# Dense experts of a two-layer decoder on one core: every product taken from coarse and fine parts, down products run beside up products

## What is computed

```python
x_attn = _layernorm(x_flat, ln_g, ln_b) @ attn_w + attn_b + x_flat
g = x_attn.reshape(2, 8, 128, 256)                      # 16 tiles of 128 tokens, 2 per expert
h = gelu(einsum('metd,edf->metf', g, w1) + b1)          # up, width 1024
y = einsum('metf,efd->metd', h, w2) + b2                # down, width 256
out = gelu(y @ next_w + next_b)                         # added to x and normalized after it
```

## Time and profile before

| | us |
|---|---|
| median of 3 runs | 2444.74 |
| lowest and highest of them | 2443.32, 2446.77 |
| profiled execution: span, its own time as far as the profile has it | 2451.3 |
| PE busy in the span | 2287.7 (93%) |
| POOL busy in the span | 1062.9 (43%) |
| stage_f in the profiled execution, first to last work | 1569.3 to 1741.2 |
| of it the opening | 1569.3 to 1596.4 |
| of it experts and tail | 1596.4 to 1741.2 |

### The profile page before, as it was taken

The page is one execution under the profiler, slowest core; times in us unless marked ns, Lnnn a source line. Parts: engine busy times, 40 slices in busy tenths (PEclk is TensorE's granted clock), DMA queues, the critical chain, the costliest instruction groups (busy, mean ns, idle before and its releaser), DMA issues.

```text
span 2451.3 us, 34108 instructions
## 1 busy us (share of the span) xinstructions
PE 2287.7 (93%) x12918; PEld 1434.3 (59%) x12918; DVE 1509.6 (62%) x2293; ACT 1106.9 (45%) x2365; POOL 1062.9 (43%) x780
## 2 busy tenths in 40 slices
PE   6999999989988999999999999999899789979998
PEld 3333343367754555554655555787666657768887
DVE  6778678457744666665666676722344566565556
ACT  1567657733322444443344444332321467643323
POOL 2446546624443788884578786333301122100000
PEclk8899999999999999999999999999899899989999
DMA  6454333232110011112010111254300601020001
GB/s 127 120 98 87 73 68 74 64 90 48 1 18 1 11 15 15 15 28 44 1 15 11 15 15 20 78 159 103 86 2 25 154 24 45 1 65 14 1 1 35
DMA packets 137613, 114.21 MB, mean 47 GB/s; under 512 B 74501, under 2 KB 114931, under 8 KB 137065
## 3 DMA queue, kind: packets, MB, share of 16 engines
q1 hardware_dynamic: 100297, 111.08, 16.7%
q0 software_dynamic: 36864, 0.15, 4.3%
q10 hardware_dynamic: 288, 0.79, 0.2%
HBM read 85.99 MB, written 13.39 MB: 41 GB/s over the span
## 4 chain that ended last, share of the span: by engine, by line
PE 73%; DMA 11%; DVE 8%; ACT 4%; issue 2%; SPq 2%; POOL 0%; ACTq 0%; DVEq 0%; POOLq 0%
PE PS L128 70%; DMA adj<-e_EE,e_IX 8%; SPq L154 2%; PE PS L1248 1%; DVE a_MX L741 1%; DVE c_MX L1896 1%; ACT a_P L847 1%; DVE g_SS L132 1%; DMA a_KS<-a_KL 1%; DMA a_r<-a_RQ 1%; PE PS L360 1%; DVE c_AC L132 1%; DVE g_st L1339 0%; ACT g_SS L1433 0%; PE PS L361 0%
## 5 line engine op out<-in xcount | busy, mean ns | idle before, releaser
L353 POOL DMA_INDIRECT adj<-e_EE,e_IX x256 | 416.9, 1629 | 400.8 <-DMA adj<-e_EE,e_IX 345.9
L1896 DVE TENSOR_REDUCE c_MX<-PS 128x2 f32<-128x1024 f32 x256 | 313.0, 1222 | 176.2 <-PE PS L128 176.2
L132 POOL TENSOR_TENSOR c_AC<-c_AC,c_P 128x1024 f32<-128x1024 f32 x145 | 364.3, 2513 | 77.6 <-DVE c_AC L132 70.5
L1993 ACT ACTIVATE c_P<-PS 128x1024 f32<-128x1024 f32 x256 | 252.0, 1026 | 214.8 <-PE PS L128 214.8
L741 DVE TENSOR_REDUCE a_MX<-PS 128x2 f32<-128x1024 f32 x256 | 303.2, 1219 | 55.3 <-PE PS L128 54.2
L847 ACT ACTIVATE a_P<-PS 128x512 f32<-128x512 f32 x512 | 270.6, 601 | 87.2 <-PE PS L128 86.4
L128 PE MATMUL PS<-c_P,c_VV 128*64 128x512 f32 x1024 | 247.7, 605 | 0.0
L137 POOL TENSOR_SCALAR e_EQ<-e_KR,e_KC 128x128 bf16<-128x128 f32 x256 | 162.8, 636 | 159.4 <-DMA e_KR<-adj_key 121.5
L128 PE MATMUL PS<-a_QS,a_KS 64*128 64x512 f32 x512 | 194.3, 461 | 20.9 <-ACT a_P L847 8.8
L128 PEld LDWEIGHTS PS<-a_QS,a_KS 64*128 64x128 f32 x512 | 84.1, 189 | 172.2 <-ACT a_P L847 96.8
L128 PE MATMUL PS<-a_KS,a_QS 48*128 48x512 f32 x512 | 171.3, 477 | 10.0 <-DMA a_QS<-a_QH 4.8
(11 more groups left out here) (496 smaller groups left out, 4589.7 us busy)
## 6 DMA issues: line engine op xcount, KB each, us to landing
e_KR<-adj_key SPq DMA_DIRECT2D x64, 256.0 KB, 3.9
f_W<-in_L_ffn_w SPq DMA_DIRECT2D x16, 1024.0 KB, 7.5
c_RB<-c_r SPq DMA_DIRECT2D x58, 128.0 KB, 2.8
g_FB<-in_fside_1x16xSxS SPq DMA_DIRECT2D x8, 616.0 KB, 8.6
a_QS<-a_QH SPq DMA_DIRECT2D x32, 128.0 KB, 3.9
adj<-e_zt SPq DMA_DIRECT2D x16, 256.0 KB, 4.2
adj<-e_EE,e_IX POOLq DMA_INDIRECT x256, 3.2
d_AJ<-adj SPq DMA_DIRECT2D x8, 512.0 KB, 9.0
```

Source lines behind the costliest of these rows:

```text
L132: return v.e.tensor_tensor(o, a, b, op)
L353: g.e.indirect_dma_start(self.adj, bass.IndirectOffsetOnAxis(ap=self.IXE[:, k:k + 1], axis=0), self.EE[:, k:k + 1], None, compute_op=ALU.a ...
L1896: v.e.reduce_max(MX[:, w % 2, :, qt, kh], bank(0, 2).rearrange("p (h n) -> p h n", h=2), AX, negate=True).then_inc(*smax_dve.up())
L1993: s.e.activation(PB[t % NP][:, :, :].rearrange("p h n -> p (h n)"), bank(2 + 2 * (t % 2), 2), ACT.Exp, scale=0.125).then_inc(*st_act.up())
```

## The change

Each fp32 product of the experts becomes three products of fp32r operands: coarse x coarse, fine x coarse, coarse x fine. Coarse is the operand cast to fp32r, fine is what is left. The coarse parts are made by casts on ACT; the fine parts by subtractions, on DVE for the activations, `W1` and `NW`, on POOL for `W2` (job `split2`). Two `h` blocks of 128 features form one job now (P = 0 to 31, four per expert), and a down job `y` P - 2 follows up job `h` P, so that down products accumulate over four jobs while up products go on. The two `o` jobs of an expert become one.

In the opening the bias add moves from DVE to POOL (`at_pool` in place of `at_dve`). The 44 `send` calls of POOL are spread over its list: one behind each of the 16 bias adds, one at each of the first 28 `y` jobs. The load of `W1` now waits for up products (`h_pe`), that of `W2` for down products (`y_pe`). The `xt` transposes of the last expert, their banks and the `landmarks` sums (job `marks`) find new places.

```diff
 (schedule)
+            if i in (8, 12):
+                yield "split1", 0, i // 4 - 2
+            if i == 16:
+                yield "split_n",
+        for P in range(34):
+            e, p = divmod(P, 4)
+            if P < 32:
+                yield "h", P
+                if p < 2:
+                    yield "split2", e, p
+                elif e < 7:
+                    yield "split1", e + 1, p - 2
+            if P == 32:
+                yield "marks", 0
+            if P >= 2:
+                yield "y", P - 2
+            if P == 33:
+                yield "marks", 1
+            if p == 2 and e:
+                yield "o", e - 1
+            if P == 26:
                 yield "root", 0
+            if 29 <= P < 33:
+                for n in range(3):
+                    yield "xt", 3 * (P - 29) + n
+        yield "o", 7
 (tensor)
             elif kind == "turn_g":
-                pe.wait_ge(at_dve, t + 1)
+                pe.wait_ge(at_pool, t + 1)
...
             elif kind == "h":
+                pe.wait_ge(w1l_dve, 2 * e + p // 2 + 1)
+                pe.wait_ge(gl_dve, 16)
+                for f in (2 * p, 2 * p + 1):
+                    parts = [(W, G, k) for k in range(2) for W, G in ((W1H, 0), (W1L, 0), (W1H, 1))]
...
             elif kind == "y":
+                pe.wait_ge(w2l_pool, 2 * e + p // 2 + 1)
+                pe.wait_ge(hl_dve, P + 1)
+                for d in range(2):
+                    parts = [(W, h, j) for j in range(2) for W, h in ((W2H, HTH), (W2L, HTH), (W2H, HTL))]
...
 (vector)
-                v.wait_ge(a_dve, t + 1)
-                v.wait_ge(rows_in, 2)
-                tt(v, TM[:, t % 4, :], TM[:, t % 4, :], AB[:, :], ALU.add).then_inc(*at_dve.up())
...
+            elif kind == "h":
+                v.wait_ge(hh_act, P + 1)
+                tt(v, HTL[P % 4][:, :, :], HT[P % 4][:, :, :], HTH[P % 4][:, :, :].bitcast(F32),
+                   ALU.subtract).then_inc(*hl_dve.up())
 (scalar)
+            elif kind == "split2":
+                s.wait_ge(w2_in[e % 2], e // 2 + 1)
+                s.e.copy(W2H[e % 2][:, fs, :], W2[e % 2][:, fs, :]).then_inc(*w2h_act.up())
 (gpsimd)
-        K.edges.send(g, 44)
+        for job in jobs:
+            kind, *a = job
+            if kind == "a":
+                g.wait_ge(rows_in, 2)
+                g.wait_ge(a_dve, t + 1)
+                tt(g, tm, tm, AB[:, :], ALU.add).then_inc(*at_pool.up())
+                K.edges.send(g, 1)
+            elif kind == "split2":
+                g.wait_ge(w2h_act, 2 * e + i + 1)
+                tt(g, W2L[e % 2][:, fs, :], W2[e % 2][:, fs, :], W2H[e % 2][:, fs, :].bitcast(F32),
+                   ALU.subtract).then_inc(*w2l_pool.up())
+            elif kind == "y" and a[0] < 28:
+                K.edges.send(g, 1)
 (sync)
-                sp.wait_ge(y_pe, 2 * (e - 1))
+                sp.wait_ge(h_pe, 8 * (e - 1))
             dma(sp, W1[e % 2][:, :, :], ...)
+            if e > 1:
+                sp.wait_ge(y_pe, 4 * (e - 1))
             dma(sp, W2[e % 2][:, :, :], ...)
```

More of the change, by code:

```diff
@@ L2152, in stage_f @@
     W2 = [sb(c, f"f_W2{i}", [128, 8, 256]) for i in range(2)]
-    HT = [sb(c, f"f_HT{i}", [128, 8, 256]) for i in range(2)]
-    YT = [sb(c, f"f_YT{i}", [128, 2, 256]) for i in range(2)]
+    W1L = [K.over(f"f_W1L{i}", f"f_W1{i}", 0, [128, 2, 1024]) for i in range(2)]
+    W2L = [K.over(f"f_W2L{i}", f"f_W2{i}", 0, [128, 8, 256]) for i in range(2)]
+    W1H = [K.over(f"f_W1H{i}", "a_QH", 8192 * i, [128, 2, 1024]) for i in range(2)]
+    W2H = [K.over(f"f_W2H{i}", "a_QH", 16384 + 8192 * i, [128, 8, 256]) for i in range(2)]
+    NW = sb(c, "f_NW", [128, 2, 256])
+    NWL = K.over("f_NWL", "f_NW", 0, [128, 2, 256])
+    NWH = sb(c, "f_NWH", [128, 2, 256], F32R)
+    HT = [sb(c, f"f_HT{i}", [128, 2, 256]) for i in range(4)]
+    HTL = [K.over(f"f_HTL{i}", f"f_HT{i}", 0, [128, 2, 256]) for i in range(4)]
+    HTH = [sb(c, f"f_HTH{i}", [128, 2, 256], F32R) for i in range(4)]
+    YTH = [sb(c, f"f_YTH{i}", [128, 2, 256], F32R) for i in range(2)]
+    YTL = [sb(c, f"f_YTL{i}", [128, 2, 256], F32R) for i in range(2)]
     TN = sb(c, "f_TN", [128, 4, 256])
@@ L2164, in stage_f @@
     cc_pe, cc_dve, sd_act, n_dve, nt_pe, nt_act = K.signals(6)
-    a_pe, a_dve, at_dve, gt_pe, gt_act = K.signals(5)
-    h_pe, h_act, y_pe, y_dve, o_pe, o_dve, gelu_act, sum_dve = K.signals(8)
+    a_pe, a_dve, at_pool, gt_pe, gt_act, gl_dve = K.signals(6)
+    w1h_act, w1l_dve, w2h_act, w2l_pool, nwh_act, nwl_dve = K.signals(6)
+    h_pe, h_act, hh_act, hl_dve, y_pe, yh_dve, yl_dve, o_pe, o_dve, gelu_act, sum_dve = K.signals(11)
     var_dve, root_act, x_dve, xt_pe, xt_act, xl_dve = K.signals(6)
-    gt_pair = [GT[:, k, :].rearrange("p (m t) -> p m t", m=2) for k in range(2)]
+    gt_pair = [[G[:, k, :].rearrange("p (m t) -> p m t", m=2) for k in range(2)] for G in (GH, GL)]
     SA = K.SA
     by_half = SA[:, :, :].rearrange("p (m e) n -> p m e n", m=2)
+    x_pair = X[:, :, :].rearrange("p (m e) d -> p m e d", m=2)
     tiles = [e + 8 * m for e in range(8) for m in range(2)]
@@ L2205, in xt_bank @@
     def xt_bank(n):
-        return 7 if n < 12 else (7, 0, 1, 2)[n - 12]
+        return (0, 1)[n % 2] if n > 13 else 7 if n < 3 else (3, 4)[n % 2]
     def tensor(_):
@@ L2241, in tensor @@
-                pe.wait_ge(cc_dve, 1)
[L2242 to L2249, removed]
-            elif kind == "y":
[L2251 to L2257, removed]
+                P, = a
@@ L2258, in tensor @@
                 ins.then_inc(*y_pe.up())
             elif kind == "o":
-                e, m = a
-                pe.wait_ge(y_dve, 2 * (e + 1))
-                pe.wait_ge(nw_in, 1)
+                e, = a
+                pe.wait_ge(yl_dve, 2 * (e + 1))
+                pe.wait_ge(nwl_dve, 1)
                 if e:
-                    pe.wait_ge(o_dve, 2 * e - 1 + m)
-                for k in range(2):
-                    ins = mm(pe, bank(5 + m)[:, 0:256], YT[e % 2][:, k, 128 * m:128 * m + 128], NW[:, k, :], k == 0, k == 1)
+                    pe.wait_ge(o_dve, e)
@@ L2267, in tensor @@
+                if e == 6:
+                    pe.wait_ge(xt_act, 3)
+                for m in range(2):
+                    parts = [(y, N, k) for k in range(2) for y, N in ((YTH, NWH), (YTH, NWL), (YTL, NWH))]
+                    for q, (y, N, k) in enumerate(parts):
+                        ins = mm(pe, bank(7)[:, 256 * m:256 * m + 256], y[e % 2][:, k, 128 * m:128 * m + 128], N[:, k, :],
+                                 q == 0, q == 5)
                 ins.then_inc(*o_pe.up())
@@ L2270, in tensor @@
                 pe.wait_ge(x_dve, n + 1)
-                if n < 13:
-                    pe.wait_ge(gt_act, 16)
+                if n < 3:
+                    pe.wait_ge(o_dve, 6)
                     if n:
                         pe.wait_ge(xt_act, n)
+                elif n < 14:
+                    pe.wait_ge(yl_dve, 14)
+                    if n > 4:
+                        pe.wait_ge(xt_act, n - 1)
                 else:
@@ L2328, in vector @@
                 v.step(v.e.reciprocal(by_half[:, :, es, 8], by_half[:, :, es, 9]))
-                for n in range(12 if r else 0, 16 if r else 6):
+                for n in range(12 if r else 0, 16 if r else 3):
                     normed(n)
[L2331 to L2334, removed]
+            elif kind == "xt":
+                n, = a
+                if n < 9:
+                    normed(3 + n)
             elif kind == "o":
[L2336 to L2340, removed]
-                v.wait_ge(gt_pe, 16)
[L2342 to L2354, removed]
+                e, = a
+                pair = TM[:, 2 * (e % 2):2 * (e % 2) + 2, :]
+                v.wait_ge(o_pe, e + 1)
+                v.wait_ge(gt_pe, 16)
+                if e > 1:
+                    v.wait_ge(sum_dve, e - 1)
+                tt(v, pair, halves(bank(7)), NBB[:, :].unsqueeze(1).broadcast_to([128, 2, 256]), ALU.add).then_inc(*o_dve.up())
+                v.wait_ge(gelu_act, e + 1)
+                tt(v, x_pair[:, :, e, :], x_pair[:, :, e, :], pair, ALU.add).then_inc(*sum_dve.up())
+                v.wait_ge(sum_dve, e + 1)
+                for i in (e, e + 8):
+                    ins = v.e.bn_stats(SA[:, i, 0:6], X[:, i, :])
+                v.step(ins)
+                for i in (e, e + 8):
+                    if i < 15:
+                        ins = v.e.bn_aggr(SA[:, i, 6:8], SA[:, i, 0:6])
+                if e == 5:
+                    ins.then_inc(*var_dve.up())
         v.wait_ge(xt_act, 12)
@@ L2383, in scalar @@
                 s.wait_ge(gt_pe, t + 1)
-                s.e.copy(GT[:, :, t * 128:t * 128 + 128], halves(bank(6 + t % 2)[:, 0:256])).then_inc(*gt_act.up())
-            elif kind == "h":
[L2386 to L2392, removed]
+                s.e.copy(GH[:, :, t * 128:t * 128 + 128], halves(bank(6 + t % 2)[:, 0:256])).then_inc(*gt_act.up())
+            elif kind == "split1":
+                e, i = a
```

(27 more changed lines are left out.)

87 lines of the change are left out of this document (55 added, 32 removed).

## The result

The changed kernel takes 2505.24 us (median of 4 runs, 2499.33 to 2513.01) where the kernel before takes 2444.85 (2443.32 to 2446.77): a ratio of 1.0237, 95% interval 1.021 to 1.0265. It is slower by 60 us, 48 were forecast; it lies inside the stated range, 2470 to 2516.

A forecast was written before the change was run, and what follows sets the result against it. POOL's chain of sends, not PE, was to bound the changed stage: stage end +51.8 us, next stage -3.7, so +48.1 on 2444.7 gives 2492.8 us. The stated range was 2470 to 2516.

The forecast's parts named there:

- The chain of sends sets the pace: Opening and experts: POOL's sends, each waiting for the previous landing, hold up work PE needs; 15.7 us per expert against PE's 13.0.
- Opening: Stage start to first up product: sixteen bias adds go at the sends' 3.4 us period; +37.6 us.
- Experts: Expert loop: four sends and two W2 subtractions on POOL, 15.7 us per expert; seven experts +109.9, loads' lateness 20 us.
- Tail: Last W2 subtraction, done at 1776.3, to stage end at 1793.0, through the last down products, statistics and closing work.
- `y` 30 and 31 with transposes 4.2: First step after the last W2 subtraction: PE runs the last two down jobs and transposes in 4.2 us.
- Next stage: Following stage: its memsets find POOL free, so PE's 3.75 us wait goes; -3.7 us, bounds 0 and -3.9.
- Signs: Trace marks: bias adds 3.3 to 3.4 us apart, subtractions 18 to 19 per expert, PE busy 65 to 70%, sends done early.
- PE's clock: Rival in the experts: stalls keep PE at the 1.2 GHz level, making it the bound; 35 us more, 2528; 8 in 100.
- Landing below 2 us: Rival on POOL's sends: a send stops waiting for the landing, period 1.83 us, PE the bound; 2431; 4 in 100.
- no-change rival: Opening and experts: send period only 2.2 to 2.3 us, time 2446; 2 in 100.
- The loads' share: Experts: weight loads delay sends by 20 us, bounds 5 and 30; rival that they are absorbed, about 2464, 6 in 100.
- PE's 23 us: Experts: fp32r matmuls take 104 us where the fp32 passes took 127, a gain only if PE stays the bound.

The follow-up runs named there:

- Runs 1 and 2: Changed kernel: first with the opening's 16 sends moved to the next stage, 2467.43 us; second with the W2 subtraction on DVE, 2472.75 us.
- run 5: Changed kernel with no sends in the opening, two per expert instead of four, the rest in the next stage; 2441.59 us.
- run 7: Changed kernel with the up products of two jobs in four done twice, 192 matmuls more, same results; 2500.93 us.
- run 6: Kernel before the change with 28 of its 44 sends in this stage and 17 in the next; 2444.55 us.
- run 4: Changed kernel with bias add and W2 subtraction on DVE, POOL only making 28 sends in one row, others in the next stage; 2437.64 us.
- run 8: Changed kernel with bias add on POOL, 28 sends in a row behind the opening, W2 subtraction on DVE; 2435.96 us.
- run 3: Changed kernel with bias add and W2 subtraction on DVE, POOL only making all 44 sends in one row; 2456.76 us.

## Why the prediction was right

**The chain of sends sets the pace: shown, up to 1756.** Runs 1 and 2 take POOL's sends out of the way of the opening and of the experts, one at a time, and each gives back its own 33 us; run 5 thins the sends in both and leaves the arithmetic on POOL, and most of both comes back; run 7 shows that up to 1756 PE was no bound.

**Opening.** Forecast 64.7 us from the start of the stage, measured 62.8. The period taken from the earlier trace rows, 3.4, was 3.39.

**Experts: right as a whole, partly by luck.** From the end of the first W2 subtraction to that of the last, 134.4 forecast, 135.4 measured (1643.2 to 1778.6). Two errors cancel. The forecast counts four sends for each of seven experts and one more, 29; the list has 27, because the first two subtractions stand together ahead of `y` 0. So the first of the seven steps, from expert 0's first subtraction to expert 1's, took 13.7 us where 18.6 were forecast. The other six took 19.5 each. There 24 periods of 3.4 and 12 subtractions at 1.05 would make 94 us, and 117 were measured: late landings took 23 us, not the 17 that fall to six steps of the 20 put in. The subtraction was not under-priced. Periods that hold one and no late landing took 4.1 to 4.4 us, 4.45 forecast; its records last 2.89 us on average, but they begin before the record of the send ahead of them has ended.

**Tail: the step that was wrong.** From the last subtraction to the end of the stage the forecast has 16.7 us, it took 23.9. The step is "`y` 30 and 31 with transposes 4.2", which starts PE on the last subtraction. PE was not waiting for it. The timeline of PE in the changed kernel shows its last wait for POOL, a wait for ACT, and the first matmul of `y` 28:

```profile
1756.29 0.58 PE L128 MATMUL PS<-f_HTH,f_W2H 128*128 128x256 f32 x1 [5.09 <-POOL f_W2L L132]
...
1767.10 0.39 PE L128 MATMUL PS<-f_GH,f_W1H 128*128 128x256 f32 x1 [1.79 <-ACT f_HT L2465]
...
1777.62 0.28 PE L128 MATMUL PS<-f_HTH,f_W2H 128*128 128x256 f32 x1
```

Expert 7's first subtraction was done at 1774.1, 3.5 us before `y` 28, its first reader; its second at 1778.6, 8.1 us before `y` 30 (1786.68). From 1756.29 on it is PE, ACT and DVE, job by job, that make the time: 46.2 us to the end of the stage. The forecast has 39.7 from there: its 1771.8 less one step of 18.6, to 1793.0. The 60 matmuls that it prices at 7.2 us per expert took 11.6 here: the first 24 were 0.21 us apart, the 1.2 GHz level, behind a stall of 5.09 us, and PE then waited 1.79 for a Gelu that stands behind job `root` 0 and two table loads on ACT:

```profile
1763.13 1.28 ACT L2478 ACT_TABLE_LOAD   x1
...
1765.27 1.28 ACT L2465 ACT_TABLE_LOAD   x1
```

The last down product ended 12.4 us behind the last subtraction. The chain of waits there (start, us, what) goes through three engines:

```profile
1780.70 0.70 DVE f_TM L132
1781.42 0.63 ACT f_TM L2473
...
1784.34 0.48 ACT f_HT L2465
1784.85 0.63 ACT f_HTH L2468
1785.50 0.69 DVE f_HTL L132
...
1789.53 1.44 PE PS L128 x12
1791.00 0.88 DVE f_YTH L137 x2
```

**Next stage.** -3.7 forecast, -6.2 measured; run 6, which moves nothing but sends, gives -6.7. More than PE's own wait of 3.75 us in the earlier trace rows went; where the rest comes from stays open.

**The sum.** The terms add to 48.1; the stage's +57.5 and -6.2 give 51.3. Of the 60 measured by the medians 9 remain. 3.6 of them are the later start of the stage, which goes with the clock of the first 400 us; what sets that clock stays open. The other 5.5 come from carrying over the distance between the profiled execution's span and the median: it was 6.6 before the change and is 1.0 after it. Small slips in the prediction's working change nothing: ACT's terms per expert add to 11.0, not 11.2, and the end behind the last statistics is 5.0 in the earlier trace rows, not 5.2.

**Signs.** Bias adds 3.4 us apart, the waits of ACT and DVE in the opening, and sends done before the stage ends came as said. Two did not: W2 subtractions were 19.5 us apart from one expert to the next, not 18 to 19, and PE was busy 78% of the experts, not 65 to 70, with its clock at 0.86.

**Rivals.** PE's clock: its sign is there (0.85 in the experts), and up to 1756 run 7 shows no price. Behind 1756 it has one: 24 matmuls at 0.21 instead of 0.12 us are 2.2 us, an estimate from their distances. Landing below 2 us: no landing in the chain of the changed kernel is that short. The no-change rival falls with it, and with it the estimate by the Trainium skill, DMA: Bandwidth & Descriptors, section on the anatomy of one DMA, whose fixed part is about 2.0 us; the shortest of these landings is 2.91. The loads' share was not absorbed: sends in the experts landed after up to 7.7 us.

**Where PE's 23 us would go.** With the sends out of the way 7 are seen (run 4 against the kernel before), 10 in run 8. In run 4 PE's busy time fell by 18 instead of 23, 6 more are idle time, and 5 are lost in the opening (3 in run 8).

## What to carry to other kernels

An engine whose queue holds DMAs that wait for one another can be a slow engine, however idle it looks: POOL was busy 43% before the change, and sixteen bias adds put between its sends came 3.4 us apart, where without the sends they came 1.5 apart. Count the periods of such a row before giving the engine work that others wait for; put the row behind the work or thin it, as in runs 5 and 8. And before shortening a stage, look for what runs beside it and ends later: run 3 shortened the stage by 7 us and lost some 17 behind it.

## What the hardware showed

A subtraction on DVE is held up by one on POOL. Timeline of the changed kernel:

```profile
1653.50 3.96 DVE L132 TENSOR_TENSOR f_HTL<-f_HT,f_HTH 128x512 fp32r<-128x512 f32 x1 [2.19 <-ACT f_HTH L2468]
1653.97 2.94 POOL L132 TENSOR_TENSOR f_W2L<-f_W,f_W2H 128x1024 fp32r<-128x1024 f32 x1
```

The tile `f_HTL` in the changed kernel and in run 2 (ns min/median/max):

```profile
L132 DVE TENSOR_TENSOR f_HTL<-f_HT,f_HTH x32: 656/692/4100, 1639.8 to 1785.5; 128x512 fp32r<-128x512 f32 x32
```

```profile
L132 DVE TENSOR_TENSOR f_HTL<-f_HT,f_HTH x32: 656/692/693, 1636.7 to 1749.5; 128x512 fp32r<-128x512 f32 x32
```

A subtraction of 0.69 us took up to 4.1 in the changed kernel, 1.18 on average; with POOL's subtractions moved to DVE, and all sends still on POOL, none took over 0.693. So POOL's arithmetic holds DVE up and its sends do not. The Trainium skill, SBUF — State Buffer, section "Who interferes with whom", says that a DVE operation with two SBUF inputs and a GpSimd operation that reads SBUF exclude each other; the trace agrees. None of the long subtractions stands in the chain of waits of the changed kernel, so there it cost the stage nothing that the chain shows.
